# A two-stage cross-attention kernel: g and phi of the second stage are replaced by the Gram matrix of the context

## The chip, the core and the metric

The kernel runs on one core of one Trainium2 chip. The core has TensorE (PE, matrix products into eight PSUM banks), VectorE (DVE), ScalarE (ACT), GpSimd (POOL) and SyncE (SP), which here issues every DMA. The metric is the device time of one execution in microseconds.

## The reference, cut to what matters

There are 16 batches; x is 256 x 512 in each, the context c 256 x 512. Stage one is single-head attention; stage two is a linear attention over channels, in which the 512 columns are the positions:

```python
# stage 1 (per batch; L = S = 256, H = 512)
q, k, v = x @ w_q.T, c @ w_k.T, c @ w_v.T
probs   = softmax(q @ k.T / sqrt(H))
x1      = x + alpha * (probs @ v) @ w_o.T
# stage 2 (CI = 128; x1 is [256 channels, 512 positions], c as well)
g     = g_w @ c + g_b            # [128, 512]
theta = theta_w @ x1 + theta_b   # [128, 512]
phi   = phi_w @ c + phi_b        # [128, 512]
y     = g @ (phi.T @ theta) / H  # reordered: (g @ phi.T) @ theta
out   = batchnorm(w_w @ y + w_b) + x1
```

Since g and phi are affine in c, g @ phi.T is g_w (c c^T) phi_w^T plus terms in the row sums of c and in the biases. c c^T is the Gram matrix, 256 x 256 and symmetric.

## The kernel before, in words

Batches go in pairs, eight pairs in all, with the index b = 0, 1 inside a pair; pair 0 and pair 7 are written out, 1 to 6 are a hardware loop. Every float32 operand of a large product is split into two float32r parts, hi (rounded, made by ScalarE) and lo (the rest, subtracted by VectorE, helper `lo`), and `product` (L255-L264) multiplies hi*hi, hi*lo and lo*hi. Weights are folded at the start: qk = w_k^T w_q and ov = alpha * w_v^T w_o.

The order of the work is written out by hand, one list of calls per engine and pair, bound by semaphores. On TensorE (L357 on): `scores(0)`, `scores(1)`, `values(0, .)`, `values(1, .)`, `g_and_phi(0, .)`, `delta(0, .)`, `g_and_phi(1, .)`, `g_phi(0)` (g phi^T in plain float32), `theta_rows(0)`, `w_g_phi(0)`, `delta(1, .)`, `g_phi(1)`, `output(0, .)`, `w_g_phi(1)`, then the four `t_tile`s of the next pair (keys times qk, their input the context transposed, cT) with `theta_rows(1)` between them, and `output(1, .)`. ScalarE (`exp`, then the hi parts) and VectorE (row maxima, lo parts, x1, out rows) follow in lists of the same shape. The context is loaded twice, as cT and as `c_raw`, and both are split.

The probabilities are transposed off TensorE: VectorE transposes 32 x 32 squares in place (`turn_squares`, L665), SP sends them to DRAM (L189), waits until they are stored, and fetches them back into the places of the transposed squares with four DMAs (L193). Each of these waits holds everything that SP would issue next.

SP's list per pair is (L213 on): loads of x for b = 0 and 1 when the outputs before are stored; the two turns of the probabilities; then, each behind a wait for the last reader, the loads of xT, cT and c for the pair after the next; then the stores of the two outputs.

Of the kernel before, what the change touches and what calls it, by code (L numbers as in the profile page):

```python
# [16 lines left out]
P = 128  # L17
# [10 lines left out]
W_B, GAMMA, BETA, MEAN, VAR, THETA_B, N_COL = 0, 2, 4, 6, 8, 10, 11  # L28
ROW_GPHI_B, ROW_GAMMA, ROW_VAR, ROW_ALPHA, N_ROW = 0, 2 * CI, 2 * CI + L, 2 * CI + 2 * L, 2 * CI + 2 * L + 1


def two_stage_cross_attention(nc, x, x_t, ctx_n, ctx_t, w_q, w_k, w_v, w_o_t, gphi_w_t, theta_w_t,
                              w_w_t, cols, rows, out):
    with ExitStack() as stack:
# [16 lines left out]
        cT = split("cT", [P, KH, 2, S])  # L51
        cn = split("cn", [P, 2, KS, H])
# [5 lines left out]
        blocks = sb("blocks", [P, 2, BLOCKS, KL * KS, SQUARE])  # L58
        moved = nc.dram_tensor("moved", [2, BLOCKS, BLOCKS, SQUARE, KL * KS * SQUARE], F32).ap()
        gphi = sb("gphi", [P, KH, 2 * CI])  # L60
        s = split("s", [P, CI])
# [4 lines left out]
        gphi_w = split("gphi_w", [P, KS, 2 * CI])  # L66
        theta_w = split("theta_w", [P, KL, CI])
        ww = split("ww", [P, L])
# [3 lines left out]
        std_row = sb("std_row", [P, L])  # L72
        bn_row = sb("bn_row", [P, L])
        std_col = sb("std_col", [P, KL])
        bn_col = sb("bn_col", [P, KL])
        out_bias = sb("out_bias", [P, KL])
        row_max = sb("row_max", [P, 2, KL])
# [9 lines left out]
        gphi_raw = setup_raw[:, 0:KS * 2 * CI].rearrange("p (k n) -> p k n", k=KS)  # L87
        theta_raw = setup_raw[:, KS * 2 * CI:KS * 2 * CI + KL * CI].rearrange("p (k n) -> p k n", k=KL)
        ww_raw = setup_raw[:, KS * 2 * CI + KL * CI:]
# [17 lines left out]
        VO_BANK = [[2, 3], [5, 6]]  # L107
        GPHI_BANK = [[7, 0], [3, 4]]
        DELTA_BANK = [[1, 2], [1, 2]]
        S_BANK = [5, 3]  # L110
        T1_BANK = [7, 6]
        THETA_BANK = [0, 1]
        OUT_BANK = [[4, 5], [4, 5]]
        LAST_OUT_BANK = [[4, 5], [7, 0]]
        TT_BANK = [7, 0, 2, 3]
        FIRST_T = [1, 2, 3, 0]
# [14 lines left out]
        c_hi, c_lo = sem("c_hi_made"), sem("c_lo_made")  # L131
        var_made, std_made = sem("var_made"), sem("std_made")
        bn_step, ww_scaled = sem("bn_step"), sem("ww_scaled")
        ww_hi, ww_lo = sem("ww_hi_made"), sem("ww_lo_made")
        idle_zeroed = sem("idle_zeroed")
        qk_done, qk_hi, qk_lo = sem("qk_done"), sem("qk_hi_made"), sem("qk_lo_made")
        ov_done, ov_hi, ov_lo = sem("ov_done"), sem("ov_hi_made"), sem("ov_lo_made")
        tT_done, tT_hi, tT_lo = sem("tT_done"), sem("tT_hi_made"), sem("tT_lo_made")
        scores_done = sem("scores_done")
# [7 lines left out]
        gphi_done, gphi_made = sem("gphi_done"), sem("gphi_made")  # L147
        delta_done, x1_made = sem("delta_done"), sem("x1_made")
        x1_hi, x1_lo = sem("x1_hi_made"), sem("x1_lo_made")
        s_done, s_hi, s_lo = sem("s_done"), sem("s_hi_made"), sem("s_lo_made")  # L150
        t1_done, t1_hi, t1_lo = sem("t1_done"), sem("t1_hi_made"), sem("t1_lo_made")
# [12 lines left out]
        def _(sp):  # L164
# [22 lines left out]
            def turn_blocks(p, b, stored_count, made_count):  # L187
                sp.wait_ge(blocks_made, made_count)
                sp.dma_start(moved[b].rearrange("j q i n -> (q i) j n"),  # L189
                             blocks[:, b].rearrange("p j x a -> p j (x a)")).then_inc(blocks_stored[b], 16)  # L190
                sp.wait_ge(blocks_stored[b], stored_count)
                for j in range(BLOCKS):
                    sp.dma_start(pT_raw[j * SQUARE:(j + 1) * SQUARE, b].rearrange("p q x a -> p q (x a)"),  # L193
                                 moved[b, j].rearrange("q i n -> i q n")).then_inc(pT_loaded[b], 16)
# [7 lines left out]
            sp.dma_start(gphi_raw[:], gphi_w_t.rearrange("(k p) n -> p k n", p=P)).then_inc(small_w_loaded, 16)  # L202
            sp.dma_start(theta_raw[:], theta_w_t.rearrange("(k p) n -> p k n", p=P)).then_inc(small_w_loaded, 16)
            sp.dma_start(ww_raw[:], w_w_t).then_inc(small_w_loaded, 16)
            sp.wait_ge(w_lo, 2 * KH)
            load_cT(0)
            sp.wait_ge(w_lo, 4 * KH)
            load_c(0)
            load_xT(0)
# [6 lines left out]
            sp.wait_ge(c_lo, 2)  # L216
            load_c(1)

            def pair(p, prefetch=True, last=False):
                two, four = counts(sp, p, 2, [1, 2, 4]), counts(sp, p, 4, [2, 3, 4])  # L220
                loads = counts(sp, p, 16, [16])
                if not (isinstance(p, int) and p == 0):
                    for b in range(2):
                        sp.wait_ge(stored[b], 16 * p)
                        load_x(p, b)
                for b in range(2):
                    turn_blocks(p, b, loads[16], two[b + 1])
                if prefetch:
                    sp.wait_ge(xT_lo, two[4])
                    load_xT(p + 2)  # L230
                    sp.wait_ge(cT_lo, two[4])
                    load_cT(p + 2)
                    sp.wait_ge(c_lo, two[4])
                    load_c(p + 2)
                sp.wait_ge(out_made, four[2])
                store(p, 0)
                if last:
                    for ct in range(KL):
                        sp.wait_ge(out_made, four[3 + ct])
                        store_tile(p, 1, ct)  # L240
                else:
                    sp.wait_ge(out_made, four[4])
                    store(p, 1)
# [12 lines left out]
        def _(pe):  # L256
# [38 lines left out]
            def t_tile(m):  # L295

                product(bank[TT_BANK[m]][:], lambda k: cut(qk, every, k, tile(m)),
                        lambda k: tuple(t[:, k].rearrange("p b s -> p (b s)") for t in cT),
                        KH).then_inc(tT_done, 1)

            def scores(b, order, last_t=None):

                for lt in range(KL):
                    dst = bank[SCORE_BANK[b]][:, lt * S:(lt + 1) * S]
                    for n, k in enumerate(order):
                        if last_t is not None and lt == 0 and n == KH - 1:
                            pe.wait_ge(tT_lo, last_t)
                        x_hi, x_lo = cut(xT, every, b, k, tile(lt))
                        t_hi, t_lo = cut(tT, every, k, b, every)
                        pe.matmul(dst, x_hi, t_hi, start=(n == 0), stop=False)  # L310
                        pe.matmul(dst, x_hi, t_lo, start=False, stop=False)  # L311
                        mm = pe.matmul(dst, x_lo, t_hi, start=False, stop=(n == KH - 1))  # L312
# [6 lines left out]
            def g_and_phi(b, half):  # L319
                for j in range(2):  # L320
                    m = 2 * half + j
                    mm = product(bank[GPHI_BANK[b][half]][:, j * 2 * CI:(j + 1) * 2 * CI],
                                 lambda k: cut(cn, every, b, k, tile(m)),
                                 lambda k: cut(gphi_w, every, k, every), KS)
                mm.then_inc(gphi_done, 1)
# [5 lines left out]
            def g_phi(b):  # L331
                for k in range(KH):
                    mm = pe.matmul(bank[S_BANK[b]][:, 0:CI], gphi[:, k, 0:CI], gphi[:, k, CI:2 * CI],  # L333
                                   start=(k == 0), stop=(k == KH - 1))
                mm.then_inc(s_done, 1)

            def w_g_phi(b):
                product(bank[T1_BANK[b]][:, 0:L], lambda k: cut(s, every, every),
                        lambda k: cut(ww, every, every), 1).then_inc(t1_done, 1)
# [5 lines left out]
            def output(b, ct, banks=OUT_BANK):  # L345
# [465 lines left out]
```

## Time and profile before

| | us |
|---|---|
| median of 3 runs | 411.24 (411.17 to 411.27) |
| profiled execution | 411.31 |
| its span, first to last instruction | 409.5 |
| TensorE busy | 401.9 |
| VectorE busy | 264.2 |
| ScalarE busy | 162.9 |

The span lacks the 1.8 us around it. TensorE's matmuls are pipelined, so a busy time near the span says that it seldom ran dry, not that it was at its peak; the distance between the starts of two products tells what one costs. The granted TensorE clock was 1.00 (2.4 GHz) throughout.

### The profile page before, as it was taken

The numbers are of one execution on the slowest core, as the hardware profiler recorded it, in microseconds if no ns is written. First come the engines' busy times: TensorE is split into PE (matmuls) and PEld (weight loads), VectorE is DVE, ScalarE is ACT, GpSimd is POOL, SyncE is SP. The second block draws the span as 40 slices with busy tenths as digits, with TensorE's granted clock in tenths as the row PEclk, the third lists the DMA queues.
The fourth block names the chain that finished last, engine by engine and source line by source line (L and its number), as shares of the span: only waits on it lengthen the run. The fifth ranks groups of instructions, "written<-read, shape, count | busy, mean of one in ns | idle before, by whom it ended". The sixth has DMA issues, their size and how long they took to land.

```text
span 409.5 us, 5832 instructions
## 1 busy us (share of the span) xinstructions
PE 401.9 (98%) x2201; PEld 347.8 (85%) x2201; DVE 264.2 (65%) x445; ACT 162.9 (40%) x296; POOL 0.7 (0%) x5
## 2 busy tenths in 40 slices
PE   8999999999999999999999999999999999999994
PEld 4888888898988988898988988888888989889893
DVE  5896767646775567746774568646675457753474
ACT  3476434425443443515343353415334153522231
POOL 0000000000000000000000000000000000000000
PEclk9999999999999999999999999999999999999999
DMA  8993452074504652064602744056511740105202
GB/s 249 360 366 142 146 175 92 10 269 138 200 2 138 196 179 102 0 235 149 230 0 77 241 105 192 0 181 203 174 56 22 251 135 1 51 0 189 70 2 102
DMA packets 29163, 55.61 MB, mean 136 GB/s; under 512 B 2656, under 2 KB 19680, under 8 KB 26080
## 3 DMA queue, kind: packets, MB, share of 16 engines
q1 hardware_dynamic: 29152, 55.46, 40.5%
q8 instruction: 7, 0.11, 0.1%
q14 instruction: 4, 0.03, 0.0%
HBM read 42.87 MB, written 12.58 MB: 135 GB/s over the span
## 4 chain that ended last, share of the span: by engine, by line
PE 97%; DVE 1%; DMA 1%; ACT 0%; issue 0%; SPq 0%
PE bank L261 26%; PE bank L262 26%; PE bank L263 25%; PE bank L290 5%; PE bank L310 4%; PE bank L312 4%; PE bank L311 4%; PE bank L333 3%; DMA cT_raw<-w_q 1%; DVE xb L717 0%; DVE tT_lo L584 0%; ACT tT_hi L442 0%; DVE theta_lo L709 0%; ACT theta_hi L442 0%; DVE vo_lo L584 0%
## 5 line engine op out<-in xcount | busy, mean ns | idle before, releaser
L584 DVE TENSOR_TENSOR tT_lo<-bank,tT_hi 128x512 fp32r<-128x512 f32 x32 | 22.0, 691 | 48.0 <-ACT tT_hi L442 48.0
L261 PE MATMUL bank<-ov_hi,cT_hi 128*128 128x512 f32 x128 | 49.9, 390 | 0.0
L262 PE MATMUL bank<-ov_lo,cT_hi 128*128 128x512 f32 x128 | 49.9, 390 | 0.0
L261 PE MATMUL bank<-cT_hi,qk_hi 128*128 128x512 f32 x128 | 49.9, 390 | 0.0
L262 PE MATMUL bank<-cT_lo,qk_hi 128*128 128x512 f32 x128 | 49.9, 390 | 0.0
L263 PE MATMUL bank<-cT_hi,qk_lo 128*128 128x512 f32 x128 | 49.8, 389 | 0.0
L263 PE MATMUL bank<-ov_hi,cT_lo 128*128 128x512 f32 x128 | 49.8, 389 | 0.0
L442 ACT ACTIVATE tT_hi<-bank 128x512 fp32r<-128x512 f32 x32 | 19.1, 598 | 49.9 <-PE bank L263 49.9
L442 ACT ACTIVATE x_hi<-xb 128x512 fp32r<-128x512 f32 x32 | 20.0, 630 | 47.7 <-DVE xb L694 47.7
L310 PE MATMUL bank<-tT_hi,xT_hi 128*128 128x256 f32 x128 | 36.3, 283 | 0.3 <-DVE tT_lo L584 0.3
L263 PE MATMUL bank<-gphi_w_hi,cn_lo 128*128 128x256 f32 x128 | 36.2, 283 | 0.0
L262 PE MATMUL bank<-gphi_w_lo,cn_hi 128*128 128x256 f32 x128 | 36.2, 283 | 0.0
L311 PE MATMUL bank<-tT_lo,xT_hi 128*128 128x256 f32 x128 | 36.2, 283 | 0.0
L312 PE MATMUL bank<-tT_hi,xT_lo 128*128 128x256 f32 x128 | 36.2, 283 | 0.0
L261 PE MATMUL bank<-gphi_w_hi,cn_hi 128*128 128x256 f32 x128 | 36.1, 282 | 0.0
L584 DVE TENSOR_TENSOR vo_lo<-bank,vo_hi 128x512 fp32r<-128x512 f32 x32 | 22.0, 686 | 19.6 <-ACT vo_hi L442 18.7
L499 ACT ACTIVATE probs<-bank,neg_max 128x256 f32<-128x256 f32 x32 | 14.9, 469 | 49.4 <-DVE neg_max L655 49.4
L442 ACT ACTIVATE vo_hi<-bank 128x512 fp32r<-128x512 f32 x32 | 19.0, 594 | 28.4 <-PE bank L263 28.3
L263 PEld LDWEIGHTS bank<-ov_hi,cT_lo 128*128 128x128 f32 x128 | 24.0, 188 | 5.1
L263 PEld LDWEIGHTS bank<-cT_hi,qk_lo 128*128 128x128 f32 x128 | 24.0, 188 | 5.1
L261 PEld LDWEIGHTS bank<-cT_hi,qk_hi 128*128 128x128 f32 x128 | 24.1, 188 | 4.8
L261 PEld LDWEIGHTS bank<-ov_hi,cT_hi 128*128 128x128 f32 x128 | 24.1, 188 | 4.8
(109 smaller groups left out, 861.5 us busy)
## 6 DMA issues: line engine op xcount, KB each, us to landing
cT_raw<-ctx_t SPq DMA_DIRECT2D x8, 1024.0 KB, 4.9
c_raw<-ctx_n SPq DMA_DIRECT2D x8, 1024.0 KB, 5.9
xT_raw<-x_t SPq DMA_DIRECT2D x8, 1024.0 KB, 4.9
xb<-x SPq DMA_DIRECT2D x16, 512.0 KB, 4.4
out<-xb SPq DMA_DIRECT2D x15, 512.0 KB, 3.7
moved<-blocks SPq DMA_DIRECT2D x16, 256.0 KB, 2.9
probs<-moved SPq DMA_DIRECT2D x64, 64.0 KB, 1.9
xb<-w_k SPq DMA_DIRECT2D x4, 256.0 KB, 4.0
```

What stands on the lines that cost most here:

```text
L261: pe.matmul(dst, ahi, bhi, start=(k == 0), stop=False)
L262: pe.matmul(dst, ahi, blo, start=False, stop=False)
L263: mm = pe.matmul(dst, alo, bhi, start=False, stop=(k == k_tiles - 1))
L290: mm = pe.matmul(bank[KH * n + m][:], lhs[a][:, k, tile(m)], rhs[b][:, k, :], start=(k == 0 and a == b), stop=(k == KH - 1 and a == 1))
L310: pe.matmul(dst, x_hi, t_hi, start=(n == 0), stop=False)
L311: pe.matmul(dst, x_hi, t_lo, start=False, stop=False)
L312: mm = pe.matmul(dst, x_lo, t_hi, start=False, stop=(n == KH - 1))
L333: mm = pe.matmul(bank[S_BANK[b]][:, 0:CI], gphi[:, k, 0:CI], gphi[:, k, CI:2 * CI], start=(k == 0), stop=(k == KH - 1))
L442: act.activation(dst, src, ACT.Identity, **more).then_inc(made, 1)
L499: e = act.activation(probs[:, b, lt], bank[SCORE_BANK[b]][:, lt * S:(lt + 1) * S], ACT.Exp, bias=neg_max[:, b, lt:lt + 1], scale=SCALE, ac ...
L584: dve.tensor_tensor(parts[1][at], src, parts[0][at].bitcast(F32), ALU.subtract).then_inc(made, 1)
```

## The change

TensorE no longer computes g and phi. At the end of a pair it computes for the next pair, from the transposed context, hi^T * [hi | lo] in two row blocks (512 and 384 columns wide; cT's parts now lie side by side in `c_sides`). ScalarE copies the cross term hi * lo out of PSUM; what is missing is its transpose and, below the diagonal, the mirrored block. VectorE transposes the squares of the cross term with the corner added, SP sends them through DRAM, and VectorE adds them back (`gram_close`). ScalarE sums the rows of c (`c_sums`); the sums stand as a 257th column. `phi_gram` multiplies phi_w with gram; its 128 x 256 result is transposed by the same way through DRAM (third turn on SP), gets phi_b times the row sums (`u_rows`), is split and multiplied by wg = w_w g_w, which `w_g_bias` makes once; `t1_rows` adds the bias term. PSUM banks are dealt out anew, and the splits of xT, cT and the order of every engine's list change.

SP's list per pair, cut:

```diff
+                sp.wait_ge(gram_blocks_made, two[2])
+                send(gram_moved[1], gram_blocks[:, 1], gram_stored[1])
+                for b in range(2):
+                    sp.wait_ge(gram_stored[b], turned[16])
+                    fetch(gram_blocks[:, b], gram_moved[b], gram_loaded[b])
                 if not (isinstance(p, int) and p == 0):
                     for b in range(2):
                         sp.wait_ge(stored[b], 16 * p)
                         load_x(p, b)
                 for b in range(2):
-                    turn_blocks(p, b, loads[16], two[b + 1])
+                    sp.wait_ge(blocks_made, two[b + 1])
+                    send(moved[b], blocks[:, b], blocks_stored[b])
+                    sp.wait_ge(blocks_stored[b], turned[16])
+                    fetch(pT_raw[:, b], moved[b], pT_loaded[b])
+                sp.wait_ge(phi_blocks_made, two[2])
+                send(phi_moved, phi_blocks[:], phi_stored)
+                sp.wait_ge(phi_stored, turned[16])
+                fetch(phi_blocks[:], phi_moved, phi_loaded)
                 if prefetch:
+                    sp.wait_ge(cT_lo, two[4])
+                    load_cT(p + 2)
+                sp.wait_ge(out_made, four[2])
+                store(p, 0)
+                if prefetch:
+                    sp.wait_ge(c_summed, four[8])
+                    load_c(p + 2)
                     sp.wait_ge(xT_lo, two[4])
                     load_xT(p + 2)
...
+                    sp.wait_ge(gram_blocks_made, two[3])
+                    send(gram_moved[0], gram_blocks[:, 0], gram_stored[0])
                     sp.wait_ge(out_made, four[4])
                     store(p, 1)
```

TensorE's new products and its list per pair:

```diff
+            def gram_rows(b, i):
+                for k in range(KH):
+                    mm = pe.matmul(bank[GRAM_BANK[b][i]][:, i * P:], cT[0][:, k, b, tile(i)],
+                                   c_sides[:, k, b].rearrange("p h s -> p (h s)")[:, i * P:],
+                                   start=(k == 0), stop=(k == KH - 1))
+                mm.then_inc(gram_done, 1)
+
+            def phi_gram(b):
+                product(bank[PHI_BANK[b]][:, 0:GW], lambda k: cut(phi_w, every, k, every),
+                        lambda k: cut(gram, every, b, k, every), KS).then_inc(phi_done, 1)
+
+            def w_g_bias():
+                for k in range(KS):
+                    pe.matmul(bank[WG_BANK][:, k * L:(k + 1) * L], g_raw[:, tile(k)], ww_raw, start=True, stop=True)
+                pe.matmul(bank[WG_BIAS_BANK][:, 0:L], g_bias[:], ww_raw, start=True, stop=True).then_inc(wg_done, 1)
...
+                product(bank[T1_BANK[b]][:, 0:L], lambda k: cut(u, every, 2 * b + k, every),
+                        lambda k: cut(wg, every, k, every), KS).then_inc(t1_done, 1)
...
+                pe.wait_ge(gram_read, two[2])
                 for st in range(KS):
                     values(0, st)
...
+                values(1, 0)
+                for b in range(2):
+                    pe.wait_ge(gram_lo, two[b + 1])
+                    phi_gram(b)
+                values(1, 1)
                 pe.wait_ge(vo_lo, four[2])
                 pe.wait_ge(pT_lo, two[1])
                 for lt in range(KL):
                     delta(0, lt)
...
+                pe.wait_ge(v_made, two[2])
                 pe.wait_ge(vo_lo, four[4])
                 pe.wait_ge(pT_lo, two[2])
                 for lt in range(KL):
                     delta(1, lt)
...
+                pe.wait_ge(cT_lo, two[4])
+                t_tile(0)
+                pe.wait_ge(x1_lo, four[2])
+                theta_rows(0)
+                t_tile(1)
+                pe.wait_ge(u_lo, p + 1)
+                pe.wait_ge(x1_lo, four[4])
+                w_g_phi(0)
+                w_g_phi(1)
+                theta_rows(1)
+                t_tile(2)
...
+                    output(0, ct)
+                t_tile(3)
...
+                    gram_rows(0, i)
...
+                    output(1, ct)
+                pe.wait_ge(out_made, four[2])
+                for i in range(KS):
+                    gram_rows(1, i)
```

ScalarE's and VectorE's lists per pair (VectorE's new steps are `gram_close`, the gram and phi squares, `u_rows`, `t1_rows`, `gram_squares`):

```diff
+                vo_part(0, 0)
+                gram_part(0)
+                gram_part(1)
+                vo_part(0, 1)
                 pT_part(0)
+                vo_part(1, 0)
+                pT_part(1)
+                vo_part(1, 1)
...
                     cT_parts(loads[32])
+                for b in range(2):
+                    for lt in range(KL):
+                        x1_part(b, lt)
+                u_part()
...
+                tT_part(2, four[7])
+                act.wait_ge(u_lo, p + 1)
+                c_sums(loads[32])
+                tT_part(3, four[8])
+                for b in range(2):
+                    for i in range(KS):
+                        cross_copy(b, i, four[4 + 2 * b + i + 1])
...
+                gram_close(0)
+                vo_part(0, 0)
+                gram_part(0)
+                gram_close(1)
+                gram_part(1)
+                vo_part(0, 1)
                 pT_part(0)
+                vo_part(1, 0)
+                phi_squares(0)
+                phi_squares(1)
+                pT_part(1)
+                vo_part(1, 1)
                 if not last:
                     cT_parts([two[3], two[4]])
+                for b in range(2):
+                    x1_rows(b)
+                    for lt in range(KL):
+                        x1_part(b, lt)
+                u_rows()
+                u_part()
...
+                tT_part(3, four[8])
+                gram_squares(0, [four[5], four[6]], two[3])
                 out_rows(1, 0)
                 out_rows(1, 1)
+                gram_squares(1, [four[7], four[8]], two[4])
```

## Rows read from the trace of the kernel before

**Rows 1.** The page: busy time of TensorE, and the chain that ended last.

```profile
PE 401.9 (98%) x2201; PEld 347.8 (85%) x2201; DVE 264.2 (65%) x445; ACT 162.9 (40%) x296; POOL 0.7 (0%) x5
...
PE 97%; DVE 1%; DMA 1%; ACT 0%; issue 0%; SPq 0%
```

**Rows 2.** TensorE's timeline: start us, us, what, idle before it.

```profile
38.10 0.28 PE L310 MATMUL bank<-tT_hi,xT_hi 128*128 128x256 f32 x1
...
85.63 0.28 PE L310 MATMUL bank<-tT_hi,xT_hi 128*128 128x256 f32 x1
...
110.79 1.05 PE L333 MATMUL bank<-gphi 128*128 128x128 f32 x8
...
131.23 0.39 PE L261 MATMUL bank<-theta_hi,t_hi 128*128 128x512 f32 x1
...
132.59 0.28 PE L310 MATMUL bank<-tT_hi,xT_hi 128*128 128x256 f32 x1
...
133.90 0.28 PE L312 MATMUL bank<-tT_hi,xT_lo 128*128 128x256 f32 x1
...
403.92 0.47 PE L261 MATMUL bank<-theta_hi,t_hi 128*128 128x512 f32 x1 [1.66 <-DVE theta_lo L709]
```

**Rows 3.** VectorE by line and form: count, busy us, mean ns, idle before.

```profile
L684 DVE TENSOR_TENSOR gphi<-bank,row 128x256 f32<-128x256 f32 x64 | 22.7, 416 | 0.8 <-PE bank L263 0.7
L584 DVE TENSOR_TENSOR tT_lo<-bank,tT_hi 128x512 fp32r<-128x512 f32 x32 | 22.0, 691 | 48.0 <-ACT tT_hi L442 48.0
...
L665 DVE STREAM_TRANSPOSE blocks<-probs 128x512 f32<-128x512 f32 x16 | 11.4, 712 | 18.4 <-ACT probs L499 18.4
...
L584 DVE TENSOR_TENSOR s_lo<-bank,s_hi 128x128 fp32r<-128x128 f32 x16 | 4.6, 289 | 13.9 <-ACT s_hi L442 13.9
```

**Rows 4.** ScalarE's timeline, then VectorE's, behind a landed transposition.

```profile
98.38 0.64 ACT L442 ACTIVATE pT_hi<-probs 128x512 fp32r<-128x512 f32 x1 [0.73 <-DMA probs<-moved]
...
102.49 0.60 ACT L442 ACTIVATE vo_hi<-bank 128x512 fp32r<-128x512 f32 x1 [2.12 <-PE bank L263]
102.99 2.00 ACT L442 ACTIVATE cT_hi<-cT_raw 128x1024 fp32r<-128x1024 f32 x2
...
99.05 0.69 DVE L675 TENSOR_TENSOR pT_lo<-probs,pT_hi 128x512 fp32r<-128x512 f32 x1 [0.60 <-ACT pT_hi L442]
...
104.07 2.36 DVE L584 TENSOR_TENSOR cT_lo<-cT_raw,cT_hi 128x1024 fp32r<-128x1024 f32 x2 [0.26 <-ACT cT_hi L442]
...
107.68 1.40 DVE L694 SCALAR_TENSOR_TENSOR xb<-bank,inv_sum,xb 128x512 f32<-128x512 f32 x2
109.18 1.29 DVE L584 TENSOR_TENSOR x_lo<-xb,x_hi 128x512 fp32r<-128x512 f32 x2
```

**Rows 5.** SP's queue in order of time; x is how many issues.

```profile
95.09 1.76 SPq L193 DMA_DIRECT2D probs<-moved  x4
...
127.11 0.33 SPq L176 DMA_DIRECT2D c_raw<-ctx_n  x1
127.98 6.46 SPq L182 DMA_DIRECT2D out<-xb  x2
...
138.56 0.38 SPq L189 DMA_DIRECT2D moved<-blocks  x1
142.92 1.75 SPq L193 DMA_DIRECT2D probs<-moved  x4
144.78 0.38 SPq L189 DMA_DIRECT2D moved<-blocks  x1
147.19 1.73 SPq L193 DMA_DIRECT2D probs<-moved  x4
```

**Rows 6.** Two stretches (clock, DMA share, GB/s last); c's load at 127.11.

```profile
20.00:32.00 12.00, 12.00 (x55) 9.93 (x54) 11.56 (x21) 9.21 (x15) 0.00 (x0) 1.00 0.93 351
128.00:134.00 6.00, 6.00 (x33) 5.18 (x33) 2.63 (x4) 1.20 (x2) 0.00 (x0) 1.00 0.82 264
...
DMA to landing us min/median/max: 6.0/6.0/6.0
```

More of the change, by code:

```diff
@@ L317, in values @@
                         lambda k: cut(ov, every, k, every), KH).then_inc(vo_done, 1)
[L319 to L325, printed above, removed]
+            def gram_rows(b, i):
+                for k in range(KH):
+                    mm = pe.matmul(bank[GRAM_BANK[b][i]][:, i * P:], cT[0][:, k, b, tile(i)],
[9 more added lines that the diff above has]
+                pe.matmul(bank[WG_BIAS_BANK][:, 0:L], g_bias[:], ww_raw, start=True, stop=True).then_inc(wg_done, 1)
             def delta(b, lt):
@@ L381, in pair @@
                     delta(0, lt)
-                pe.wait_ge(c_lo, two[2])
-                for half in range(2):
-                    g_and_phi(1, half)
+                pe.wait_ge(v_made, two[2])
                 pe.wait_ge(vo_lo, four[4])
-                pe.wait_ge(gphi_made, four[2])
-                g_phi(0)
-                pe.wait_ge(x1_lo, four[2])
-                theta_rows(0)
-                pe.wait_ge(s_lo, two[1])
-                if first:
-                    pe.wait_ge(ww_lo, 1)
-                w_g_phi(0)
                 pe.wait_ge(pT_lo, two[2])
@@ new lines, in u_rows @@
+                def u_rows():
+                    dve.wait_ge(phi_loaded, landed[16 * BLOCKS])
+                    phi_b = row[:, ROW_PHI_B:ROW_PHI_B + CI].rearrange("p (q a) -> p q a", q=BLOCKS)
+                    for b in range(2):
+                        for k in range(KS):
+                            at = phi_blocks[:, :, b * KS + k]
+                            dve.scalar_tensor_tensor(out=at, in0=phi_b, scalar=gram_raw[:, b, k, S:S + 1], in1=at,
+                                                     op0=ALU.mult, op1=ALU.add).then_inc(u_made, 1)
@@ L724, in pair @@
                 turn_squares(1)
-                if not last:
-                    for b in range(2):
-                        xT_part(b, two[b + 3])
-                invert_sums(0)
-                vo_parts(0)
-                invert_sums(1)
-                pT_part(0)
-                vo_parts(1)
+                for b in range(2):
+                    invert_sums(b)
+                if first:
+                    lo(wg, wg_hi, 1, (every,), bank[WG_BANK][:].rearrange("p (k l) -> p k l", k=KS), wg_lo)
@@ new lines, in pair @@
+                if first:
+                    dve.wait_ge(wg_bias_made, 1)
+                if last:
+                    for b in range(2):
+                        t1_rows(b)
+                    for b in range(2):
+                        t1_part(b)
+                    theta_part(0)
+                    theta_part(1)
+                    for b in range(2):
+                        for ct in range(KL):
+                            out_rows(b, ct)
+                    return
+                tT_part(0, four[5])
@@ L748, in pair @@
+                theta_part(0)
+                tT_part(1, four[6])
+                for b in range(2):
+                    t1_rows(b)
+                for b in range(2):
+                    t1_part(b)
+                theta_part(1)
+                for b in range(2):
+                    xT_part(b, two[b + 3])
+                tT_part(2, four[7])
                 out_rows(0, 0)
-                t1_part(1)
                 out_rows(0, 1)
-                if not last:
-                    tT_part(0, four[5])
-                    c_part(0, two[3])
-                    tT_part(1, four[6])
-                    c_part(1, two[4])
```

453 lines of the change are left out of this document (242 added, 211 removed).

## The prediction

> **What bounds the kernel now.** I read the page first: TensorE is busy 98% of the span and the chain of work that ended last runs over it for 97% [rows 1]. Then TensorE's timeline, for the period of one pair and the pitch of its products [rows 2]. The first scores product of a pair starts at 85.63, of the next at 132.59: 46.96 us. Six products of 512 columns start from 131.23 to 132.59, 0.227 us each; eleven of 256 columns from 132.59 to 133.90, 0.119 us each. A pair has 144 of the wide and 102 of the narrow ones: 32.64 + 12.14 = 44.8 us; the other 2.2 us are the two `g_phi` in plain fp32 (eight instructions in 1.05 us [rows 2]) and small gaps. So TensorE's own work sets the period and other engines have slack. Last I read SP's queue [rows 5], since the change puts most of its new steps there.
>
> T is the time since a pair's first scores product, T' the same in the pair that follows.
>
> **What it takes off TensorE.** Away: 48 products of `g_and_phi`, 6 of `w_g_phi`, and the `g_phi`: 54 x 0.119 + 2.2 = 8.6 us. New: `gram_rows`, 8 of 512 columns and 8 of 384 (between the two pitches, 0.173): 3.2 us; `phi_gram`, 12 of 258, and `w_g_phi`, 12 of 256: 24 x 0.119 = 2.9 us. Per pair 6.1 against 8.6: 44.4 us instead of 47.0, if nothing waits. Ideal ends: scores 5.7, `values(0)` 11.2, `values(1,0)` 13.9, both `phi_gram` 15.3, `values(1,1)` 18.0, `delta(0)` 20.8, `delta(1)` 23.6, then t_tile(0), theta(0), t_tile(1) to 30.3, then `w_g_phi` and all that follows, 14.15 us of products.
>
> **What it adds elsewhere.** VectorE per pair, by its steps of 512, 256 and 128 columns [rows 3]: 31 steps of 512 columns (with the new splits of gram and u) at 0.70, 21.7; the four splits of cT and xT at 1.18 [rows 4], 4.7; 4 of `gram_close`, 4 of t1 at 0.42 and 6 transposes of 256 columns, which have no row: half of the 0.71 of 512, at most the whole; taken 0.36: 5.5; six adds of the Gram corners and four `u_rows` of 128 columns at 0.29, 2.9; a few of one or two columns. In all some 35 us of 44.4 (37 by the upper bound of the transposes): not the bound by itself, but more than before (`gphi_rows` and the splits of c and s go) and one strict order.
> ScalarE gets four copies out of PSUM, two gram splits, a u split and four sums of c (a 512-column pass with an accumulator; no row; 0.63 without, with a read behind it at most 0.85). The sums lie between the third and the fourth t-tile, 3.4 us apart, so 2.5 as well as 3.4 us of them are covered. `pT_part(1)` now stands ahead of the last vo split and of the cT splits on ScalarE: if its data are late, both wait behind it, and all of x1 behind them on VectorE.
> SP gets three more turns through DRAM, each a send of 256 KB, a wait, and four fetches. One turn costs SP 2.41 us from send to stored when nothing lies ahead (144.78 to 147.19) and 1.75 us for the four fetches; data are used 3.3 us after the first fetch is issued (95.09 to 98.38) [rows 4, 5]. Before, SP ran two such turns a pair, with the send of b0 at T = 5.97 (138.56).
>
> **The new path through SP.** At the top of each pair SP waits for the second Gram transposes, sends them, waits until they are stored (call that moment G, in T), fetches, issues both loads of x, and only then sends the probabilities of b0. From G: fetches 1.75, load x 0.8, send at G+2.55; it has 1 MB of x just ahead. Before, with about half of that ahead, send to stored took 4.36 (138.56 to 142.92) and the send itself came later after the loads; I take 4.55: fetch b0 at G+7.1, send b1 at G+8.9, fetch b1 at G+11.2, landed at D = G+14.5 (3.3 later).
> From D by the rows behind a landing [rows 4]: pT_hi at once, pT_lo 0.67 later; ScalarE turns to vo_hi and then to cT_hi (0.50 behind it), whose lo parts end 3.44 after it starts (102.99 to 106.43): D+4.5. Then x1 on VectorE: 2.79 us from the first `x1_rows` to the second lo part (107.68 to 110.47), and again 2.7 for b=1: D+9.9. `u_rows` four at about 0.25: D+10.9. u_hi and u_lo, 0.63 and 0.69, with their handovers 1.4: u is ready at D+12.35. `w_g_phi` can't start earlier, and 14.15 us of products follow: the period is D+26.5 = G+41.0. delta(1) waits too (vo_lo at D+2.05). Without a wait `w_g_phi` starts at 30.3, so the cover lasts while G is under 3.5.
>
> **How late is G?** TensorE's last 14.15 us fix the tail. outputs(0) end 6.9 after `w_g_phi` starts, `out_rows(0)` at 9.1, the sums of c at 9.0. So at T' = -5.0 SP issues, one behind the other, store 0 (0.5 MB), c (1 MB) and xT (1 MB); then Gram b0 (0.25), store 1 (0.5) at T' = 0.4, and at T' = 1.4 Gram b1 (0.25): 3.25 MB ahead of it; by the code before, xT and cT were loaded in mid-pair. First bytes come 0.9 after the issue. Store 0 with c: 1.57 MB at 264 GB/s, the rate when just these two ran together (128 to 134) [rows 6], 5.95 us; xT 1.05 MB at the 351 GB/s of loads alone (20 to 32) [rows 6], 3.0 us; the last 1.05 MB, writes, no row alone; by the same 351, 3.0. From -4.1: +7.85, with the receipt G = 8.0. Bounds: everything at 351, G = 6.4; everything at 264, 9.8. If the Gram send goes ahead of the rest, G = 1.4 + 2.41 = 3.8.
> Which order holds? c, issued 0.87 before the store, took 6.0 us to land [rows 6] where its bytes alone are 3.0 + 0.9: the store slowed it but did not pass it. So I take it that a send issued last lands last, with some mixing. The Trainium skill ("DMA: Bandwidth & Descriptors", Queues, rings and completion order) says that one issuing engine has one ring on each DMA engine, consumed in ring order, though completion is not strictly in order; by it the Gram send is last and G is 8, and without it 3.8 stays open. The row bears it out only in part, since it shows c slowed by what came after it.
>
> **The sum.** P = 8.0 + 41.0 = 49.0, 2.1 longer than before, for pairs 1 to 6 (pair 6 still has the loads for pair 7 ahead of it). Start: t-tiles end at 38.10 [rows 2] as before, then 3.2 of Gram: 41.3. Pair 0: c for pair 1 (2.9 behind 0.9) is issued some 1.2 us into the scores, then both Gram sends: G about 7; no loads of x at its top, so b0 goes out alone (2.41): D = G+11.6 = 18.6, under its own work 44.4 + 1.3 for `w_g_bias` (three plain fp32 products of 256 columns, each like two of `g_phi`: 1.0 to 1.6): 45.9. Pair 7: no loads of c and xT before it, only store 1 and Gram b0: G about 4.4, D = 19.1; without cT parts u_lo at D+9.9, then `w_g_phi`, both theta, their split (1.5), output(1) from D+15.8 = 34.9; the last output before started at 403.92, 5.6 before the end [rows 2]: 40.5. 41.3 + 45.9 + 6 x 49.0 + 40.5 = 421.7; the profiled execution took 411.31 for a span of 409.5 (1.8 around it): **423.5 us**. The median 411.24 is the same within 0.1. Bounds of G, 6.4 and 9.8: P 47.4 and 50.8, 414 and 434.
>
> **Rivals.**
> *The small send passes the big loads, or the loads finish sooner (faster).* G is 3.8 to 5; P = 44.8 to 46; 129.5 + 6P gives 399 to 406, middle 403. For it: c and a store did mix. Against: no send in the trace passed a load. It decides at G = 5.9 (P = 46.97), where the time is that of before.
> *The chain is shorter and TensorE stays the bound (faster).* P = 44.4 and 395: VectorE's steps from D would have to be 2 us shorter at G near 4. For it: before, the same waits cost TensorE nothing. Against: 35 us of VectorE steps in strict order.
> *Both sizes worse (slower).* G near 9.8, or delta(0) late too, since its pT lands at G+10.4: 434.
> *No change.* G within 0.1 of 5.9: a crossing, not a case with a reason.
>
> **Numbers.** Forecast 414 to 434: 0.57; worse still 0.04; passing send 0.26; TensorE-bound 0.09; near the crossing 0.04. What a measurement can tell from no change is about 0.2%, 0.8 us. Faster 0.35, same 0.04, slower 0.61. The range, 399 to 431, leaves out the TensorE-bound case and the last tenth above; the likeliest's own is 414 to 434.
>
> **What would show it.** TensorE's busy time falls but it waits three times in each inner pair: before delta(0), before delta(1) some 2 us, before `w_g_phi` 0.7. The longest waits of SP are on the stored Gram and probability sends; the Gram b1 send lands 6 us or more after its issue, against 2.4 to 4.4 for sends before. Pair 0 takes 46, pairs 1 to 6 49, from one scores start to the next. Wrong if the Gram send lands in 3 us while c and xT are in flight; if the period is 46 or less; if the longest wait of TensorE is for a tile that comes of no DMA; or if the granted clock, 1.00 all through now, falls after the stalls, which I don't price.

## The result and the profile after

| | before | after |
|---|---|---|
| median, us (lowest to highest) | 411.25 (411.17 to 411.35) | 440.10 (439.29 to 444.08) |
| ratio | | 1.072, 95% interval 1.065 to 1.079 |
| profiled execution, us; span | 411.31; 409.5 | 439.35; 437.6 |
| mean granted clock of TensorE | 1.00 | 0.984 |

The changed kernel is 29 us slower. 423.5 was forecast, with 431 as the upper end: the sign was right, the size was less than half of what it is.

The page of the kernel after: busy times, TensorE's granted clock in 40 slices, the chain that ended last, ScalarE's waits for landed probabilities, and two DMA issues (count, KB each, us to landing).

```profile
PE 400.7 (92%) x1967; PEld 331.7 (76%) x1967; DVE 292.0 (67%) x567; ACT 189.5 (43%) x385; POOL 1.8 (0%) x7
...
PEclk9999999999899998999989999999999999999989
...
PE 37%; DMA 28%; DVE 11%; SPq 11%; ACT 6%; issue 5%; DVEq 0%; ACTq 0%
...
L492 ACT ACTIVATE pT_hi<-probs 128x512 fp32r<-128x512 f32 x16 | 10.1, 631 | 68.1 <-DMA probs<-moved 68.1
...
gram_moved<-gram_blocks SPq DMA_DIRECT2D x16, 256.0 KB, 5.9
...
moved<-blocks SPq DMA_DIRECT2D x16, 256.0 KB, 2.5
```

TensorE was busy 98% of the span and 97% of the chain [rows 1]; now it is 92% and 37%, and its busy time hardly fell, from 401.9 to 400.7 us, though it has 234 instructions fewer. Part of it runs at a lower clock (the 8s), so a busy microsecond holds less work: in experiment 3 the same 1967 products are busy for 392.6 us. DMA and SP's queue hold 39% of the chain. One pair shows how. SP's queue of the kernel after in pair 1, whose first scores product starts at 90.53 (T = 0):

```profile
85.10 0.36 SPq L205 DMA_DIRECT2D out<-xb  x1
85.50 0.43 SPq L199 DMA_DIRECT2D c_raw<-ctx_n  x1
85.98 0.78 SPq L193 DMA_DIRECT2D xT_raw<-x_t  x1
88.96 0.38 SPq L211 DMA_DIRECT2D gram_moved<-gram_blocks  x1
90.80 0.34 SPq L205 DMA_DIRECT2D out<-xb  x1
91.94 0.37 SPq L211 DMA_DIRECT2D gram_moved<-gram_blocks  x1
95.15 4.66 SPq L216 DMA_DIRECT2D gram_blocks<-gram_moved  x8
100.36 0.97 SPq L202 DMA_DIRECT2D xb<-x  x2
101.46 0.39 SPq L211 DMA_DIRECT2D moved<-blocks  x1
107.04 1.75 SPq L216 DMA_DIRECT2D probs<-moved  x4
...
gram_moved<-gram_blocks SPq DMA_DIRECT2D x1, 256.0 KB, 5.2
```

The last line is the send issued at 91.94 alone, that of the second Gram blocks (b1): 5.2 us to landing. The page's median of 5.9 mixes it with the first (b0): over pairs 1 to 6, b1 takes 5.2 to 5.6 and b0 6.2 to 6.6.

The probabilities of b0 are sent at T = 10.9 (5.97 before [rows 5]), and from this send to the fetch pass 5.6 us where 4.36 had passed. TensorE's timeline and one row of ScalarE's, the same pair (in brackets the idle time before and what ended it; `u` is the split, turned and biased result of `phi_gram`):

```profile
90.53 0.28 PE L349 MATMUL bank<-tT_hi,xT_hi 128*128 128x256 f32 x1
...
111.98 0.47 PE L302 MATMUL bank<-vo_hi,pT_hi 128*128 128x512 f32 x1 [2.94 <-DVE pT_lo L766]
...
126.85 0.39 PE L302 MATMUL bank<-wg_hi,u_hi 128*128 128x256 f32 x1 [0.30 <-DVE u_lo L801]
...
141.35 0.28 PE L349 MATMUL bank<-tT_hi,xT_hi 128*128 128x256 f32 x1
...
114.47 0.63 ACT L492 ACTIVATE pT_hi<-probs 128x512 fp32r<-128x512 f32 x1 [2.88 <-DMA probs<-moved]
```

The pair takes 50.8 us where 46.96 were [rows 2]. Its last probabilities land at T = 23.9 (D), `w_g_phi` starts 12.4 later, and 14.5 us of products follow. The clock in it, by stretches of the kernel after (us; busy us of PE, PEld, DVE, ACT, POOL; then granted clock, DMA share, GB/s):

```profile
86.00:97.00 11.00, 11.00 (x75) 10.30 (x74) 7.11 (x17) 3.15 (x9) 0.00 (x0) 1.00 1.00 342
...
113.00:114.00 1.00, 1.00 (x4) 0.84 (x3) 0.35 (x2) 0.00 (x0) 0.00 (x0) 0.59 0.50 142
114.00:115.00 1.00, 1.00 (x4) 0.72 (x3) 0.00 (x0) 0.53 (x1) 0.00 (x0) 0.50 0.82 232
115.00:116.00 1.00, 1.00 (x4) 0.60 (x2) 0.86 (x2) 1.00 (x3) 0.00 (x0) 0.50 0.12 34
```

Two things are read here. Around the Gram sends the DMA engines are full (share 1.00 for 11 us, 342 GB/s). And about 1.2 us after TensorE has resumed from the 2.94 us wait the clock is halved, to 1.2 GHz, for some 3 us: four products a microsecond, all "busy". The page's busy time hides that.

The last pair of the kernel after: SP's send of b0 and its fetch, then TensorE's wait for u, then the clock.

```profile
399.21 0.43 SPq L211 DMA_DIRECT2D moved<-blocks  x1
406.22 0.80 SPq L216 DMA_DIRECT2D probs<-moved  x2
...
423.60 0.43 PE L302 MATMUL bank<-wg_hi,u_hi 128*128 128x256 f32 x1 [4.85 <-DVE u_lo L801]
...
425.00:426.00 1.00, 1.00 (x7) 1.00 (x7) 0.48 (x1) 0.35 (x1) 0.00 (x0) 0.50 0.00 0
```

### The profile page after: what moved, and what is told of

Its sections match the earlier page's. It is cut to its first block, busy times and chain, and to the rows that moved or that the text cites. A ratio compares the mean times of both kernels' runs of the same rounds, so it can differ in the third digit from the quotient of the medians.

```text
span 437.6 us, 5814 instructions
## 1 busy us (share of the span) xinstructions
PE 400.7 (92%) x1967; PEld 331.7 (76%) x1967; DVE 292.0 (67%) x567; ACT 189.5 (43%) x385; POOL 1.8 (0%) x7
## 4 chain that ended last, share of the span: by engine, by line
PE 37%; DMA 28%; DVE 11%; SPq 11%; ACT 6%; issue 5%; DVEq 0%; ACTq 0%
DMA moved<-blocks 14%; DMA gram_moved<-gram_blocks 10%; PE bank L302 9%; SPq L216 9%; PE bank L303 9%; PE bank L304 9%; PE bank L361 5%; PE bank L331 5%; DMA probs<-moved 4%; DVE x_lo L660 2%; DVE xb L812 2%; ACT x_hi L492 2%; DVE c_sides L660 2%; DVE phi_blocks L796 2%; SPq L202 1%
## 5 line engine op out<-in xcount | busy, mean ns | idle before, releaser
L302 PE MATMUL bank<-c_sides,qk_hi 128*128 128x512 f32 x128 | 51.0, 399 | 0.0
L303 PE MATMUL bank<-c_sides,qk_hi 128*128 128x512 f32 x128 | 50.8, 397 | 0.0
L302 PE MATMUL bank<-ov_hi,c_sides 128*128 128x512 f32 x128 | 50.7, 396 | 0.0
L304 PE MATMUL bank<-ov_hi,c_sides 128*128 128x512 f32 x128 | 50.6, 395 | 0.0
L303 PE MATMUL bank<-ov_lo,c_sides 128*128 128x512 f32 x128 | 50.5, 394 | 0.0
L304 PE MATMUL bank<-c_sides,qk_lo 128*128 128x512 f32 x128 | 50.4, 394 | 0.0
L302 PE MATMUL bank<-vo_hi,pT_hi 128*128 128x512 f32 x64 | 27.7, 433 | 24.0 <-DVE vo_lo L660 11.9
L557 ACT ACTIVATE probs<-bank,neg_max 128x256 f32<-128x256 f32 x32 | 14.9, 469 | 39.5 <-DVE neg_max L747 39.5
L303 PEld LDWEIGHTS bank<-c_sides,qk_hi 128*128 128x128 f32 x128 | 24.4, 191 | 5.8
L304 PEld LDWEIGHTS bank<-c_sides,qk_lo 128*128 128x128 f32 x128 | 24.4, 190 | 5.8
L302 PEld LDWEIGHTS bank<-c_sides,qk_hi 128*128 128x128 f32 x128 | 24.3, 190 | 5.7
L361 PE MATMUL bank<-c_sides 128*128 128x512 f32 (+1 forms) x128 | 28.4, 365 | 0.0
L304 PEld LDWEIGHTS bank<-ov_hi,c_sides 128*128 128x128 f32 x128 | 24.1, 188 | 5.6
L303 PEld LDWEIGHTS bank<-ov_lo,c_sides 128*128 128x128 f32 x128 | 24.1, 188 | 5.0
```

The lines of the kernel that those rows point to most:

```text
L302: pe.matmul(dst, ahi, bhi, start=(k == 0), stop=False)
L303: pe.matmul(dst, ahi, blo, start=False, stop=False)
L304: mm = pe.matmul(dst, alo, bhi, start=False, stop=(k == k_tiles - 1))
L361: mm = pe.matmul(bank[GRAM_BANK[b][i]][:, i * P:], cT[0][:, k, b, tile(i)], c_sides[:, k, b].rearrange("p h s -> p (h s)")[:, i * P:], sta ...
L557: e = act.activation(probs[:, b, lt], bank[SCORE_BANK[b]][:, lt * S:(lt + 1) * S], ACT.Exp, bias=neg_max[:, b, lt:lt + 1], scale=SCALE, ac ...
```

## The experiments

**The question.** The theory is the prediction's: the chain through SP (Gram sends behind the loads, then the probabilities behind the fetches and the loads of x) sets the period. The rivals: that VectorE's steps in strict order bound it, whatever SP does; that the Gram send is slow only because it stands behind the loads in SP's own queue; that the halved clock is the loss. A pair's period is taken from one first scores product to the next; the ratio is to the kernel before on the same chip.

| run | what differs | median us | ratio (95%) | inner pairs, us |
|---|---|---|---|---|
| after | | 440.10 | 1.072 (1.065 to 1.079) | 49.4 to 51.2 |
| e1_loads_mid | loads of c and xT in mid-pair | 425.19 | 1.031 (1.028 to 1.035) | 50.7, then 47.3 to 47.8 |
| e2_x_late | loads of x behind the probabilities | 409.55 | 0.995 (0.994 to 0.997) | 47.0, then 45.2 to 45.8 |
| e3_both | e1 and e2 | 407.22 | 0.990 (0.987 to 0.993) | 45.2 |
| e4_gram_on_act | Gram sends on ScalarE's queue | 445.70 | 1.082 (1.080 to 1.085) | 49.6 to 52.5 |
| e5_fill_waits | idle products in TensorE's waits | 438.74 | 1.067 (1.065 to 1.068) | 49.4 to 51.6 |
| e6_best | e3, and two repairs | 401.80 | 0.977 (0.975 to 0.979) | 45.2 |
| e7_best_fill | e6, and idle products in one wait | 400.54 | 0.973 (0.972 to 0.974) | 45.2 |
| e8_flat_parts | e3, parts of cT laid out apart | 409.83 | 0.997 (0.996 to 0.998) | 45.7 |

**1. The loads of c and xT leave the tail (e1_loads_mid).**

```diff
                 fetch(phi_blocks[:], phi_moved, phi_loaded)
+                if not last and not (isinstance(p, int) and p == 0):
+                    sp.wait_ge(c_summed, four[4])
+                    load_c(p + 1)
+                    sp.wait_ge(xT_lo, two[2])
+                    load_xT(p + 1)
...
                 store(p, 0)
-                if prefetch:
-                    sp.wait_ge(c_summed, four[8])
-                    load_c(p + 2)
-                    sp.wait_ge(xT_lo, two[4])
-                    load_xT(p + 2)
```

> The loads of c and xT leave the tail of a pair and are issued by SP in the middle of the next, behind the phi fetches; nothing else moves. Queue theory: the second Gram send, issued 1.4 us into a pair, no longer has 2 MB ahead of it; it is stored at 4.5 to 5 us instead of 8.1, the probabilities land 3 us earlier and an inner pair takes 47 us instead of 50.3: some 420 us in all. Rival 'VectorE's strict order sets the pair': the landing moves and the pair stays at 50: 439. Rival 'bandwidth': mid-pair the loads meet the phi turn instead, and u comes late: 430 or more.

The page, and SP's queue in the pair that starts at 141.5, of this kernel:

```profile
gram_moved<-gram_blocks SPq DMA_DIRECT2D x16, 256.0 KB, 2.6
...
142.90 0.37 SPq L211 DMA_DIRECT2D gram_moved<-gram_blocks  x1
...
147.63 0.94 SPq L202 DMA_DIRECT2D xb<-x  x2
148.68 0.38 SPq L211 DMA_DIRECT2D moved<-blocks  x1
154.77 1.76 SPq L216 DMA_DIRECT2D probs<-moved  x4
```

Without the 2 MB of loads the second Gram send lands in 2.6 to 2.7 us instead of 5.2 to 5.6, and in pair 2 the probabilities of b0 go at T = 7.2 instead of 10.0, 2.8 us earlier. In pairs 4 to 6 they go 2.5 to 2.6 us earlier and the period falls by 2.1 to 2.3, since the send of b0, behind the 1 MB of x, still takes 5.7 to 6.3 us to be stored. In pairs 2 and 3, which had a stretch of half clock that is gone here, it falls by 3.3 and 3.4. Pair 1 stays at 50.7: its send of b0 goes at T = 9.0, and half clock follows. That, and 47.3 to 47.8 instead of 47 in the others, is why 425 was measured and not the 420 expected. So the loads in the tail are a part of the cause, worth 15 us when they alone are moved.

**2. The loads of x go behind the probabilities (e2_x_late).**

```diff
-                if not (isinstance(p, int) and p == 0):
-                    for b in range(2):
-                        sp.wait_ge(stored[b], 16 * p)
-                        load_x(p, b)
                 for b in range(2):
                     sp.wait_ge(blocks_made, two[b + 1])
                     send(moved[b], blocks[:, b], blocks_stored[b])
                     sp.wait_ge(blocks_stored[b], turned[16])
                     fetch(pT_raw[:, b], moved[b], pT_loaded[b])
+                if not (isinstance(p, int) and p == 0):
+                    for b in range(2):
+                        sp.wait_ge(stored[b], 16 * p)
+                        load_x(p, b)
```

> Only SP's two loads of x move, from ahead of the probabilities' sends to behind their last fetch. Queue theory: the send of b0 is stored in 2.5 us instead of 5.6 and comes 0.9 earlier, so the last probabilities land 4 us earlier; Gram's send stays late (8.1 us). An inner pair takes 46.5 us: 415. Rival 'VectorE's order': 439. If x then comes late for x1, the pair takes 49.

SP's queue of this kernel, pair 2, whose scores start at about 137.1:

```profile
138.50 0.37 SPq L211 DMA_DIRECT2D gram_moved<-gram_blocks  x1
141.98 3.77 SPq L216 DMA_DIRECT2D gram_blocks<-gram_moved  x8
145.98 0.38 SPq L211 DMA_DIRECT2D moved<-blocks  x1
148.30 1.73 SPq L216 DMA_DIRECT2D probs<-moved  x4
```

The Gram sends are as slow as in the changed kernel (the page has 5.9 us for them too), yet the time falls by 30.5 us and below that of the kernel before. Send to fetch of b0 is 2.3 us, not 5.6, and it goes 1.1 us earlier (T = 8.9 against 10.0 in pair 2 of the changed kernel): 4.4 us off the chain, which brings it near TensorE's own work. With that goes the half clock of this pair, so its period falls by 5.4, and the kernel ends 5 us under the 415 expected. This one place, two loads ahead of a small send that the chain waits for, is the difference between 7% slower and even (0.5% faster).

**3. Both (e3_both).**

> Both moves of SP's issues together. Queue theory: the last probabilities land at 16 to 17 us of a pair, under TensorE's own work, and a pair takes TensorE's 44.5 to 45 us with no wait over 0.5 us: 398 to 401 us in all, 2.5% to 3% under the kernel before the change. Rival 'VectorE's order': not under 425. Rival 'clock': with the waits the half clock goes too, so this one can't tell it from the queue.

The page's chain of this kernel, and SP's queue in pair 2:

```profile
PE 87%; DVE 4%; DMA 3%; ACT 2%; SPq 2%; issue 1%; DVEq 0%; POOL 0%; ACTq 0%; POOLq 0%
...
137.46 0.37 SPq L211 DMA_DIRECT2D gram_moved<-gram_blocks  x1
137.98 3.93 SPq L216 DMA_DIRECT2D gram_blocks<-gram_moved  x8
142.04 0.38 SPq L211 DMA_DIRECT2D moved<-blocks  x1
144.41 1.73 SPq L216 DMA_DIRECT2D probs<-moved  x4
```

TensorE is the chain again, and between 90 and 360 us it is busy for all of the 270 us at a granted clock of 1.00. All six inner pairs take 45.2. The 398 to 401 us expected are missed, since pair 0 (48.9) and the last (43.2) keep waits of their own, which experiment 6 takes up, and since TensorE's own work is 45.2 and not 44.4 (experiment 7). The two moves are worth 14.9 and 30.5 us alone but 32.9 together: each shortens the same chain, and below TensorE's work nothing more is to be had. The VectorE rival falls here: its order and its steps are those of the kernel after, and nothing waits for them in an inner pair.

**4. The Gram sends on another queue (e4_gram_on_act).** ScalarE issues them as soon as the transposes are made; SP only waits for their receipt and fetches.

```diff
+            def send_gram(b, count):
+                act.wait_ge(gram_blocks_made, count)
+                act.dma_start(gram_moved[b].rearrange("j q i n -> (q i) j n"),
+                              gram_blocks[:, b].rearrange("p j x a -> p j (x a)")).then_inc(gram_stored[b], 16)
```

> The Gram sends are issued by ScalarE, on its own DMA queue, at the same points; the loads of c and xT stay in SP's queue in the tail. If a send is late because SP's queue is taken in the order of issue, it is now stored at 4 to 5 us; if the DMA engines' bandwidth is what it waits for, at 7 to 8 as before. The fetches behind it stay in SP's queue behind the loads, so the whole gains less than e1: 428 to 436 by the first, 438 to 442 by the second.

ScalarE's issue in this kernel, the stretch around it, the page's row of all 16 sends, what the DMA engines moved from 192.4 to 196.5 by queue (q1 is SP's, q10 ScalarE's), and the time to landing of the send issued at 192.47:

```profile
192.47 0.37 ACTq L515 DMA_DIRECT2D gram_moved<-gram_blocks  x1
...
190.00:200.00 10.00, 10.00 (x70) 9.50 (x69) 6.61 (x17) 2.78 (x9) 0.00 (x0) 1.00 1.01 340
...
gram_moved<-gram_blocks ACTq DMA_DIRECT2D x16, 256.0 KB, 5.5
...
q1 hardware_dynamic: 183, 1.37, 99.1%
...
gram_moved<-gram_blocks ACTq DMA_DIRECT2D x1, 256.0 KB, 7.5
```

The page's median, 5.5 us instead of 5.9, is of a mixture. In pairs 1 to 6 the b1 sends take 5.2 to 5.5 us, on SP's queue 5.2 to 5.6; the b0 sends take 6.2 to 7.6, on SP's queue 6.2 to 6.6. So no send is faster on its own queue, and those of b0, up to 7.6 in pairs 2 to 5, are slower. There the loads of x come 0.9 to 1.3 us later in the pair than in the changed kernel and everything behind them follows, and the kernel takes 445.7 us where 438 to 442 had been expected for this case; its clock falls further too, to 0.966. The order within SP's queue is thus not what delays the send.

The trace also tells what is late. The send of 192.47 has a queue to itself, q10, and until 196.5 no byte of it has moved: q1, with the loads of c and xT and a store, has every packet. Its first packet starts 4.1 us after the issue, where that of the first Gram send, which is issued before the load of c for pair 1 and lands in 2.3 us, starts 0.9 after. The Trainium skill ("DMA: Bandwidth & Descriptors", Queues, rings and completion order) says that a DMA engine takes turns between the queues, packet by packet, but also that the increment of a DMA's semaphore lands only after every earlier write of that engine, across its queues. The first would have let the small send through, and for those 4 us the trace does not show it, though from 196.5 on packets of both queues run side by side. The second would hold back the receipt alone, but here the bytes themselves are late. Why they start only when the loads are nearly through (that of xT lands at 198.1) stays open.

**5. Idle products in the waits (e5_fill_waits).** Products of a zeroed bf16 tile stand before both `delta` and, in the last pair, before `w_g_phi`. They leave the DMA chain as it is.

```diff
+            def fill(n, count):
+                pe.wait_ge(probs_made, count)
+                for _ in range(n):
+                    pe.matmul(bank[0][:], idle[:, 0:P], idle[:], start=True, stop=True)
```

> The changed kernel with idle bf16 products put into TensorE's waits (seven ahead of each delta wait, 19 ahead of the last pair's wait for u; they write a PSUM bank that is free). If the half clock behind the waits costs what is missing in my sum, the granted clock stays at 1.00, the pairs that had a half-clock stretch (50.8 to 51.2) come down to the 49.4 to 50 of the others and the last pair loses 2 us: 433 to 435 in place of 440. Rival 'the clock falls where nobody waits for TensorE': 440. The waits for the probabilities stay in both.

The page's clock, and three pairs (90 to 241) of this kernel:

```profile
PEclk9999999999999999999999999999999999999998
...
90.00:241.00 151.00, 146.73 (x736) 118.62 (x738) 100.56 (x196) 65.30 (x135) 0.00 (x0) 1.00 0.49 156
```

The clock stays at full speed, pairs 2 and 3 take 49.7 and 49.9 instead of 50.9 and 51.2, the last pair 44.1 instead of 45.15. By the medians 1.4 us are won, less than the 4.8 us over which the changed kernel's own times spread, and by the spans of the profiled executions 1.6; 433 to 435 had been expected. What the clock cost is better seen inside the pairs. From the landing D to the end, pairs 2 and 3 are 0.9 and 1.0 us shorter than in the changed kernel and the last is 1.5 us shorter; in pairs 2 and 3 TensorE reached `w_g_phi` at D + 13.4 without a wait for u, here at D + 12.4. Pair 1 gained nothing (51.6 against 50.8): half clock or not, u was what it waited for, at D + 12.4 in both, and its send of b0 took 6.2 us here against 5.6. So the halved clock is the smaller part of the miss: 1.6 us net, 3.4 from D on in the three pairs that gained; the rest of the 29 is the chain's.

**6. A better version (e6_best, e7_best_fill).** e3 leaves two places. Pair 0 still has the load of c for pair 1 ahead of its Gram sends: it moves to mid-pair. And the last pair waits 4.67 us for u: there u is made before the last split of x1, and `theta_rows(0)` stands before `w_g_phi`.

```diff
-            sp.wait_ge(c_summed, 4)
-            load_c(1)
             sp.wait_ge(gram_blocks_made, 1)
...
                 if last:
+                    pe.wait_ge(x1_lo, four[2])
+                    theta_rows(0)
                     pe.wait_ge(u_lo, p + 1)
...
                 if last:
+                    x1_rows(0)
+                    x1_part(0, 0)
+                    x1_part(0, 1)
+                    x1_rows(1)
+                    u_rows()
+                    x1_part(1, 0)
+                    u_part()
+                    x1_part(1, 1)
+                    theta_part(0)
```

> Both moves of e3, and two more: c for pair 1 is loaded in the middle of pair 0, and in the last pair u is made before the last split of x1, with theta_rows(0) ahead of w_g_phi. Queue theory: pair 0 goes from 48.7 to 46 us, since its Gram sends no longer stand behind c; the last pair from 43.3 to 41. Inner pairs stay at 45.2. 401 to 403 us. If pair 0 stays at 48.7, its delay is not the load of c but VectorE's start.

e7 adds eight idle products between `theta_rows(0)` and `w_g_phi` of the last pair.

> e6 with eight idle products in the last pair's wait for u. If the half clock falls behind that wait in e6 and costs the last products 1 to 1.5 us, they come back; with the clock whole in e6 the two are the same within 0.5 us.

TensorE's timeline and a stretch of e6:

```profile
388.38 0.38 PE L301 MATMUL bank<-wg_hi,u_hi 128*128 128x256 f32 x1 [3.01 <-DVE u_lo L805]
...
388.40:392.00 3.60, 3.60 (x16) 3.31 (x17) 2.73 (x6) 1.13 (x3) 0.00 (x0) 0.61 0.00 0
```

and the same of e7:

```profile
385.41 1.67 PE L405 MATMUL bank<-idle 128*128 128x512 bf16 x7
387.71 0.38 PE L301 MATMUL bank<-wg_hi,u_hi 128*128 128x256 f32 x1 [0.63 <-DVE u_lo L811]
...
387.70:392.00 4.30, 4.29 (x24) 3.57 (x24) 3.32 (x7) 1.86 (x4) 0.00 (x0) 1.00 0.00 0
```

Pair 0 falls from 48.9 to 46.5, near the prediction's pair 0 without a wait (45.9); the last pair from 43.2 to 41.0 and, with the idle products, to 38.8. Behind a 3 us wait the clock had gone to 0.61 over the next 3.6 us; behind the idle products (seven of the eight are in the trace) it stayed at 1.00. Of the 2.2 us between these two executions 1.5 lie behind the start of `w_g_phi` and are the clock's; the other 0.6 come before it, where the turn of phi happened to land earlier, and the medians of e6 and e7 are 1.3 us apart. The version beats the kernel before by 2.7% (2.6 to 2.8).

**7. The layout of cT (e8_flat_parts).** In e3 an inner pair takes 45.2 where the sum of TensorE's work had said 44.4. The 48 products `bank<-c_sides,qk` of one pair start 0.233 us apart on the mean, those of `bank<-cT,qk` before 0.227; over the 96 products that read c a pair, that is 0.5 of the 0.8 us. This kernel is e3 with hi and lo of cT in blocks of their own instead of side by side.

```diff
-        c_sides = sb("c_sides", [P, KH, 2, 2, S], F32R)
-        cT = c_sides[:, :, :, 0], c_sides[:, :, :, 1]
+        c_sides = sb("c_sides", [P, 2, KH, 2, S], F32R)
+        cT = c_sides[:, 0], c_sides[:, 1]
```

> e3 with hi and lo of cT each in one block as before the change, in place of side by side for each k and b; the second Gram row block becomes 512 columns wide for it (8 x 128 columns more a pair, 0.43 us). In e3 products that read c_sides start 0.232 us apart, others of 512 columns 0.227. If the interleaved layout costs that, the pitch falls to 0.227, and the pair stays at 45.1 to 45.2; if not, the pair takes 45.6.

The inner pair is 45.7, half a microsecond more (the second Gram block is 512 wide in it, not 384), and the 48 products still start 0.233 us apart, so the interleaving is not the cause. It stays open.

## Why the prediction was wrong

Its steps in the order of a pair, against the changed kernel's profiled execution. G, D and T are the prediction's; moments of storing are by the trace's semaphores.

| | forecast | pair 1 | pairs 2, 3 | pairs 4 to 6 |
|---|---|---|---|---|
| Gram b1 stored, G | 8.0 | 6.6 | 6.9, 7.0 | 6.6 to 6.7 |
| b0 sent | 10.55 | 10.9 | 10.0, 10.0 | 9.5 to 9.7 |
| its send to stored | 4.55 | 5.6 | 5.6, 5.7 | 5.4 to 5.9 |
| last landing, D | 22.5 | 23.9 | 23.1, 23.3 | 22.5 to 23.1 |
| D to `w_g_phi` | 12.35 | 12.4 | 13.4, 13.5 | 12.4 |
| products behind it | 14.15 | 14.5 | 14.4, 14.4 | 14.5 |
| pair | 49.0 | 50.8 | 50.9, 51.2 | 49.4 to 50.0 |

- **What bounds it, the path, the order**: right. TensorE waits for pT, then for vo_lo, and in some pairs for u; the longest waits of SP and ScalarE are for the DMAs named.
- **Send of b0 to stored, 4.55**: wrong, and this is the step that failed. It took 5.4 to 5.9 in the inner pairs and 7.0 in the last. I took the row from before, where about half as much lay ahead, and added 0.2. The prediction's own numbers would have done better: 1 MB of x at 351 GB/s is 3.0 us, behind it the 2.41 of a send alone [rows 5], 5.4 in all. From the send of b0 to D pass 12.9 to 13.4 us where the forecast has 11.95, most of it this term.
- **G = 8.0**: too late by 1.0 to 1.4, near the bound for everything at 351 GB/s (6.4): the forecast took the store and c at the 264 of before, and the DMA engines moved 342 GB/s around the Gram sends. The sign "lands 6 us or more after its issue" did not come, b1 takes 5.2 to 5.6; but the rival in which the small send passes the loads (G of 3.8 to 5) is out. In pair 1 the next term hid it: from G to the send of b0 pass 4.4 us and not 2.55, since SP is still issuing the first four fetches, one of which takes it 1.4 us, and has the other four before it. That the send then goes near T = 10.55 is luck. In pairs 2 to 6 it takes 2.7 to 3.1, and the early G hides half or more of what comes late behind it.
- **D to u, 12.35**: right, 12.4 wherever TensorE waited for u. **The tail, 14.15**: 14.5, partly the slower pitch of experiment 7.
- **The clock**: named as a thing that would make it wrong and not priced. In pairs 1 to 3 the mean clock is 0.97, in the last 0.96. By e5 it cost 0.9 and 1.0 us in pairs 2 and 3, nothing in pair 1, and 1.5 in the last.
- **Pair 0, 45.9**: wrong by 3.0. The forecast let it be bound by TensorE with D = 18.6; c lay ahead of both Gram sends, which took 6.5 and 6.3 us (issued at 43.41 and 44.51), so G was 9.2 and not 7, the send of b0 came at T = 12.0 instead of G + 2.55 = 9.6, and D is 22.0.
- **The last pair, 40.5**: wrong by 4.65. D was 21.3, not 19.1 (the 7.0 us above; why it is 7.0 and not 5.6 stays open). The rest lies behind D: `w_g_phi` starts at D + 9.9 as said, but from it to the end pass 14.0 us where the forecast leaves 11.5; the half clock behind the 4.85 us wait is 1.5 of that, and no run here shows the rest.

The sum of the misses: start 0.3, pair 0 3.0, six inner pairs 301.9 against 294.0, so 7.9, last pair 4.65: 15.9 us, from 421.7 to the span of 437.6. In the inner pairs G came early and the steps behind it late, and late won. The range was too narrow for that: both bounds had been given for G alone, none for the send of b0, for pair 0 or for the last pair.

The reason behind the loss is shown by e2 and e3: not the Gram matrix, of whose 2.6 us a pair off TensorE 1.75 are there once nothing waits (45.2 against 46.96), but the order of SP's steps around it.

## What to carry to other kernels

When a change puts a round trip through DRAM on the path, list each transfer issued in the ten microseconds before each small send: every megabyte ahead of a send that has still to move costs it about 3 us at 350 GB/s (an estimate from the 351 of rows 6; 1 MB of x took the send of b0 from 2.3 us to 5.6), whether both are on SP's queue or the send on ScalarE's, and this for each send of the chain, not only for the new one. Move large loads behind the last small send that something waits for; here this moved two pairs of lines and turned 7% slower into 1% faster. And price a new wait of TensorE twice, for its length and for the products at half clock that can follow it (0.9 to 1.5 us each time that it cost anything here), or fill it with idle products.

## What the runs showed of the hardware that was not expected

- A 256 KB send issued on ScalarE's own queue while SP's loads filled the DMA engines (340 GB/s) took 5.2 to 7.6 us to land, on SP's queue 5.2 to 6.6 (pairs 1 to 6 of e4 and of the changed kernel), and 2.3 to 2.7 with no load ahead. On its own queue the first of its packets started 4.1 us after the issue, against 0.9 with no load ahead.
- In the changed kernel the granted clock fell to its lower level, 1.2 GHz, for some 3 us after TensorE's waits of 2.94 and 4.85 us, in e6 after one of 3.01, each time within 1.3 us after it had resumed. Shorter waits do not settle it by their length: in pair 3, with two of 1.92 and 1.95 us, the clock fell; in pair 4, with 1.93 and 1.72, it stayed at 1.00. The rows of the changed kernel's pairs 3 and 4 (219 to 222 and 263 to 271):

```profile
217.59 0.47 PE L302 MATMUL bank<-vo_hi,pT_hi 128*128 128x512 f32 x1 [1.95 <-DVE vo_lo L660]
219.00:222.00 3.00, 3.00 (x8) 2.32 (x8) 2.90 (x4) 1.23 (x2) 0.00 (x0) 0.50 0.25 46
...
263.00:271.00 8.00, 5.44 (x23) 4.25 (x24) 5.94 (x11) 3.46 (x5) 0.00 (x0) 1.00 0.34 98
```

- Idle bf16 products in the wait of e6 kept the clock at 2.4 GHz and gave 1.5 us back behind it.
- Products of 512 columns do not all start 0.227 us apart: those of keys and values, which read `c_sides`, did so at 0.232 to 0.233, in the layout of e8 as well, while the last six of a pair before the scores (`theta_hi,t_hi` and its partners) start 0.227 apart in both kernels, but 0.231 to 0.232 in two pairs of the changed kernel. Interleaving of the parts is not the cause.
